# Mamba block and mixture of experts on one core: a new front and end, and a new order in the middle of each chunk

## The reference

```python
x = x + _layernorm(mamba(_layernorm(x)))
x = x + _layernorm(ffn(_layernorm(x)))

# mamba: 512 inner channels, 16 states, 4 taps
xz = x @ W_in; x_in, z = split(xz)
u = silu(causal_conv4(x_in) + conv_b)
dt_lr, Bm, Cm = split(u @ W_xproj)              # 16, 16, 16
delta = softplus(dt_lr @ W_dt + b_dt)
h_t = exp(delta_t * A) * h_{t-1} + delta_t * u_t * B_t   # per channel and state
y = (sum over n of h * C + D_skip * u) * silu(z)
out = y @ W_out

# ffn: shared gate/up/down (256), and 8 experts of 128 with top-2 softmax weights
routed = sum over e of coef_e * (silu(x@gate_e) * (x@up_e)) @ down_e
```

## Time and profile before

| what | us |
|---|---|
| median of three runs (lowest, highest) | 2349.79 (2345.92, 2350.08) |
| the profiled execution | 2349.13 |
| its span, first to last instruction | 2347.3 |
| from the start to the first scan | 58.8 |
| the sixteen chunks of scans | 58.8 to 2247.5 |
| after the last scan | 99.8 |
| VectorE busy | 2151.0 (92%) |
| TensorE busy | 2069.7 (88%) |
| GpSimd busy | 1970.5 (84%) |
| ScalarE busy | 1643.2 (70%) |

### The profile page before, as it was taken

How to read it: one execution, slowest core, us unless ns; L and a number is a source line. 1 busy time by engine, 2 the same in 40 slices (tenths; PEclk the granted TensorE clock), 3 DMA queues, 4 the chain that set the end, 5 groups by cost and what they waited for, 6 DMA issues and landing times. The chain is left out here.

```text
span 2347.3 us, 30291 instructions
## 1 busy us (share of the span) xinstructions
PE 2069.7 (88%) x9216; PEld 1345.5 (57%) x9216; DVE 2151.0 (92%) x3048; ACT 1643.2 (70%) x2489; POOL 1970.5 (84%) x1630
## 2 busy tenths in 40 slices
PE   5678989999989899989989899999989899897967
PEld 2345565656656565665656556565656656565544
DVE  1999999999999999999999999999999999998950
ACT  4657777777777776777767687677778777775632
POOL 4677898989989898998979899898989989798844
PEclk8759999999999999999999999999999999997989
DMA  4111221111121111212121211221112121111201
GB/s 129 41 37 41 64 64 51 59 60 59 55 64 54 60 55 59 64 55 60 59 56 50 68 60 54 60 61 56 51 55 72 55 60 50 55 55 46 76 14 46
DMA packets 92947, 134.28 MB, mean 57 GB/s; under 512 B 12000, under 2 KB 42976, under 8 KB 92784
## 3 DMA queue, kind: packets, MB, share of 16 engines
q1 hardware_dynamic: 92784, 132.34, 18.8%
HBM read 123.13 MB, written 9.18 MB: 56 GB/s over the span
## 5 line engine op out<-in xcount | busy, mean ns | idle before, releaser
L817 DVE TENSOR_TENSOR_SCAN h<-d_a,carry,d_bu 128x512 f32<-128x512 f32 x1024 | 1261.0, 1267 | 52.9 <-ACT d_a L623 46.2
L1062 POOL TENSOR_TENSOR d_bu<-delta_u,b_rows 128x1024 f32<-128x1024 f32 x512 | 1202.5, 2359 | 4.6 <-issue 0.3
L623 ACT ACTIVATE d_a<-delta,a_neg 128x512 f32<-128x512 f32 x1024 | 697.4, 689 | 500.7 <-DVE h L817 495.2
L457 PE MATMUL ht<-ident,h 128*128 128x128 f32 x4096 | 611.5, 295 | 104.4 <-DVE y_t L827 97.2
L457 PEld LDWEIGHTS ht<-ident,h 128*128 128x128 f32 x4096 | 506.4, 151 | 337.4 <-issue 121.5
L827 DVE SCALAR_TENSOR_TENSOR y_t<-ht,c_t,y_t 128x512 f32<-128x512 f32 x896 | 621.2, 735 | 2.8 <-PE ht L457 2.4
L532 PE MATMUL ring<-x_t,w_gate_sb 128*128 128x512 f32 x640 | 324.8, 633 | 21.3 <-ACT delta L782 18.0
L559 PE MATMUL dn<-w_down_sb,up_hidden 128*128 128x256 f32 x1280 | 302.9, 379 | 1.7 <-POOL up_hidden L1122 1.7
L539 PE MATMUL ring<-x_t,w_up_sb 128*128 128x512 f32 x640 | 292.5, 600 | 12.4 <-ACT silu_gate L716 12.2
L1117 POOL TENSOR_TENSOR up_hidden<-silu_gate,up_hidden 128x512 f32<-128x512 f32 x160 | 204.3, 1277 | 109.0 <-ACT up_hidden L720 76.9
L559 PEld LDWEIGHTS dn<-w_down_sb,up_hidden 128*128 128x128 f32 x1280 | 236.0, 190 | 60.0 <-issue 31.8
(11 more groups left out here) (121 smaller groups left out, 2013.0 us busy)
## 6 DMA issues: line engine op xcount, KB each, us to landing
b_rows<-b_rows_hbm SPq DMA_DIRECT2D x256, 256.0 KB, 3.5
coef_rows<-coef_rows_hbm SPq DMA_DIRECT2D x128, 256.0 KB, 3.5
xa<-L_attn_x_in SPq DMA_DIRECT2D x16, 512.0 KB, 5.0
xr<-L_attn_x_in SPq DMA_DIRECT2D x16, 512.0 KB, 5.1
out<-xr SPq DMA_DIRECT2D x16, 512.0 KB, 2.9
w_in_sb<-L_attn_W_in_in SPq DMA_DIRECT2D x1, 1024.0 KB, 6.3
w_gate_sb<-L_ffn_experts_gate_in SPq DMA_DIRECT2D x2, 512.0 KB, 4.8
w_up_sb<-L_ffn_experts_up_in SPq DMA_DIRECT2D x2, 512.0 KB, 5.7
```

Source lines behind the costliest of these rows:

```text
L457: last = nc.tensor.transpose(HT[q % HTS][:, j * P:(j + 1) * P], H[:, (NS * c + n) % HS, j, a * P:(a + 1) * P], IDN[:, :])
L623: nc.scalar.activation(DA[i % DAS][:, :], DL[:, r, j, :], ACT.Exp, scale=ANEG[:, j, n:n + 1]).then_inc(ex.sem, 1)
L817: nc.vector.tensor_tensor_scan(H[:, (NS * s + n) % HS, j, :], DA[(n * J + j) % DAS][:, :], BU[:, (2 * n + j // 2) % 4, j % 2, :], CARRY[:, ...
L1062: nc.gpsimd.tensor_tensor(BU[:, (2 * n + h) % 4, :, :], DU[:, 2 * h:2 * h + 2, :], BB[:, n % 2, :].unsqueeze(1).to_broadcast([P, 2, T]), A ...
```

## The change

- **Start.** TensorE no longer waits for the constants at the start but makes 32 products of the identity with itself (`WARM`) as soon as the identity is made; the wait for the constants' loads stands ahead of the preparation of chunk 0. ScalarE's exp and VectorE's negation of A_log move there too. The statistics and the normalisation of the first xa need none of it. GpSimd's `before_chunk(0)` moves behind the first rstd.
- **Chunk 0's preparation.** All four z tiles are made in slot 9, in turn in the two down banks (two in slots 58 and 60 in the ring before), and all SiLUs stand together in slot 14. The taps of the fourth group are added by VectorE (`add_first_taps`) and not by GpSimd. The second chunk's xa is normalised ahead of the first softplus (slot 27, was 50).
- **Every chunk.** The gates of pair 2 (f = 2 and 3) are both in slot 20, ahead of the coefficients' transposes in that slot; those go to DN[1] and no longer to the ring, and the first down product waits for their copy. ScalarE copies x_dbl and the coefficients one slot sooner (18, 20). Pairs 2, 3 and 4 start in slots 20, 30, 40 (22, 32, 42), the softplus groups in 28 and 38 (30, 40), two of the statistics in 24 and 34 (26, 36), the mean in 44 (42).
- **End.** Chunk 14's output is normalised at the start of lo = 16, ahead of ScalarE's last states. For chunk 15 VectorE adds each quarter once it is normalised, and SyncE stores each quarter by itself.

```diff
-        PAIR_AT = (12, 22, 32, 42, 50)
+        PAIR_AT = (12, 20, 30, 40, 50)
+        GATE_AT = (12, 13, 20, 20, 30, 31, 40, 41, 50, 51)
-        DL_PE, DL_ACT = (28, 29, 38, 39), (30, 30, 40, 40)
-        XA_STATS, XA_MEAN, XA_RSTD, XA_NORM, XT_PE, XT_ACT = (16, 16, 26, 36), 42, 47, 50, 61, 62
+        DL_PE, DL_ACT = (26, 27, 36, 37), (28, 28, 38, 38)
+        XA_STATS, XA_MEAN, XA_RSTD, XA_NORM, XT_PE, XT_ACT = (16, 16, 24, 34), 44, 47, 50, 61, 62
-        SILU_FIRST = {14: SILU[14] + SILU[60][:2], 60: SILU[60][2:]}
+        SILU_FIRST = {14: SILU[14] + SILU[60]}
+        WARM = 32
...
         def gate_slot(f):
-            return PAIR_AT[f // 2] + f % 2
+            return GATE_AT[f]
         def up_slot(f):
-            return gate_slot(f) + 3
+            return PAIR_AT[f // 2] + f % 2 + 3
         def hf_slot(f):
-            return gate_slot(f) + 5
+            return PAIR_AT[f // 2] + f % 2 + 5
-        MIDDLE = ([("xd", 1, 0, 0), ("cf", -1, 0, 1)], [("dl", 1, 0, 0), ("dl", 1, 1, 1)],
+        MIDDLE = ([("xd", 1, 0, 0)], [("dl", 1, 0, 0), ("dl", 1, 1, 1)],
...
+                    if lo == CHUNKS + 1 and t == 0:
+                        for a in range(NT):
+                            sp.wait_ge(tail.sem, a + 1)
+                            sp.dma_start(tokens(out, r, half - 1)[:, a, :], XR[:, s % 2, a, :]).then_inc(out_st.sem, 16)
...
         def _(pe):
-            pe.wait_ge(consts.sem, 1)
-            pe.wait_ge(const_ld.sem, CONST_LOADS)
             pe.wait_ge(ident_made.sem, IDENT_MADE)
+            for i in range(WARM):
+                nc.tensor.matmul(HT[i % HTS][:, 0:P], IDN[:, :], IDN[:, :], start=True, stop=True)
...
+                if lo == -1:
+                    pe.wait_ge(const_ld.sem, CONST_LOADS)
...
                 if t == CF_PE:
                     pe.wait_ge(rt.sem, rt.at(c))
-                    pe.wait_ge(*ring_user_before(s, lo, "cf", 0))
-                    bank = ring_bank("cf", 0)
+                    pe.wait_ge(x1t.sem, x1t.at(c))
+                    bank = DN[1]
...
                 if f == 0:
                     pe.wait_ge(rt.sem, rt.at(c))
+                    pe.wait_ge(cff.sem, cff.at(c))
...
-                    if t == Z_PE[j]:
-                        if j < 2:
+                    if t == (Z_PE[j] if lo >= 0 else Z_PE[0]):
+                        if lo < 0 and j >= 2:
+                            pe.wait_ge(z_raw.sem, z_raw.at(c, j - 1))
+                        elif j < 2:
+                            pe.wait_ge(sz.sem, sz.at(s, j + 3))
                             pe.wait_ge(resid["o"].sem, resid["o"].at(s - 1, 2 * j + 2))
+                        bank = z_bank(j) if lo >= 0 else DN[j % 2]
...
         def _(act):
-            act.wait_ge(const_ld.sem, CONST_LOADS)
-            nc.scalar.activation(ANEG[:, :, :], ANEG[:, :, :], ACT.Exp).then_inc(a_exp.sem, 1)
-            act.wait_ge(consts.sem, 1)
+            act.wait_ge(zeroed.sem, 1)
+                    if lo == -1 and t == 0:
+                        act.wait_ge(const_ld.sem, CONST_LOADS)
+                        nc.scalar.activation(ANEG[:, :, :], ANEG[:, :, :], ACT.Exp).then_inc(a_exp.sem, 1)
+                        act.wait_ge(consts.sem, 1)
+                    if lo == CHUNKS and t == 0:
+                        normed_y(s - 2)
-                    if exists(lo - 2) and t == 2:
+                    if exists(lo - 2) and lo != CHUNKS and t == 2:
                         normed_y(s - 2)
-                    if exists(lo + 2) and t == XA_NORM:
+                    if exists(lo + 2) and t == (XA_NORM if lo != -1 else DL_ACT[0] - 1):
                         normed("xa", s + 2, XA, XA)
-                if t == CF_PE + 1:
+                if t == CF_PE:
                     act.wait_ge(full["cf"].sem, full["cf"].at(c))
-                if t == XD_PE + 1:
+                if t == XD_PE:
                     act.wait_ge(full["xd"].sem, full["xd"].at(c))
...
+                    if lo == CHUNKS + 1 and t == 0:
+                        for a in range(NT):
+                            dve.wait_ge(norm["y"].sem, norm["y"].at(s - 2, a + 1))
+                            nc.vector.tensor_tensor(XR[:, s % 2, a, :], XR[:, s % 2, a, :], YN[:, a, :], ALU.add)\
+                              .then_inc(tail.sem, 1)
+                    if lo == -1 and t == POOL_CONV:
+                        add_first_taps(s + 1, o, POOL_J)
...
+            def add_first_taps(c, o, j):
+                nc.vector.tensor_tensor(U[:, o, j, 0:TAPS - 1], U[:, o, j, 0:TAPS - 1], HEAD[:, j, :], ALU.add)\
+                  .then_inc(conv_last.sem, 1)
+                for i in range(TAPS - 1):
+                    k = TAPS - 2 - i
+                    back = TAPS - 1 - k
+                    dve.wait_ge(conv_last.sem, conv_last.at(c, i + 1))
+                    nc.vector.tensor_tensor(U[:, o, j, back:], U[:, o, j, back:], YD[:, k, back:], ALU.add)\
+                      .then_inc(conv_last.sem, 1)
...
-                    if prep and t == POOL_CONV:
+                    if prep and lo >= 0 and t == POOL_CONV:
                         add_taps(s + 1, o, POOL_J)
-                    if exists(lo + 2) and t == HEAD_POOL:
+                    if exists(lo + 2) and lo > -2 and t == HEAD_POOL:
+                        before_chunk(s + 2, r)
+                    if lo == -2 and t == XA_RSTD + 1:
+                        pool.wait_ge(const_ld.sem, CONST_LOADS)
                         before_chunk(s + 2, r)
```

More of the change, by code:

```diff
@@ L163, in mamba_moe_kernel @@
         shift = {w: stage(f"shift_{w}", n) for w, n in dict(xa=2, o=2, x1=2, y=2).items()}
-        stream = stage("stream", 1)
+        stream, tail = stage("stream", 1), stage("tail", NT)
         scan, add_c, carry = stage("scan", NS * J), stage("add_c", (NS - 2) * NT), stage("carry_s", NS)
@@ L252, in mamba_moe_kernel @@
         ring_free = {"yd": (yd, 1), "xt": (xt, 1), "xin": (conv, TAPS), "z": (sz, 1),
-                     "gt": (tg, 1), "up": (up, 1), "cf": (cff, 1), "xd": (xd, 1), "ct": (ct, 1),
+                     "gt": (tg, 1), "up": (up, 1), "xd": (xd, 1), "ct": (ct, 1),
                      "dl": (softplus, 1)}
@@ L271, in ring_user_before @@
                 before, part, kb, bank_before = RING_USE[at]
-                if bank_before == bank and 0 <= lo - back + part < CHUNKS:
+                first = 1 if before == "z" else 0
+                if bank_before == bank and first <= lo - back + part < CHUNKS:
                     if before == "xin" and kb == POOL_J:
@@ L379, in body @@
                         sp.dma_start(XA[:, :, :], following).then_inc(xa_ld.sem, 16)
-                    if exists(lo - 2) and t == Y_POOL + 2:
+                    if lo == CHUNKS + 1 and t == 0:
+                        for a in range(NT):
+                            sp.wait_ge(tail.sem, a + 1)
+                            sp.dma_start(tokens(out, r, half - 1)[:, a, :], XR[:, s % 2, a, :]).then_inc(out_st.sem, 16)
+                    if exists(lo - 2) and lo != CHUNKS + 1 and t == Y_POOL + 2:
                         result, added = tokens(out, r, half - 1), stream.at(s - 2)
@@ L399, in _ @@
                 body(s, s, s % 2, s // 2)
-            sp.wait_ge(out_st.sem, out_st.at(CHUNKS - 1))
+            sp.wait_ge(out_st.sem, out_st.at(CHUNKS - 2) + NT * 16)
         IDENT_MADE = 2 + E
@@ L575, in prep_part @@
                             pe.wait_ge(*ring_user_before(s, lo, "z", j))
+                        bank = z_bank(j) if lo >= 0 else DN[j % 2]
                         for k in range(KM):
-                            last = nc.tensor.matmul(z_bank(j)[:, :], WIN[:, k, DI + j * P:DI + (j + 1) * P],
+                            last = nc.tensor.matmul(bank[:, :], WIN[:, k, DI + j * P:DI + (j + 1) * P],
                                                     XT[:, k, :], start=(k == 0), stop=(k == KM - 1))
@@ L721, in ffn_part @@
                           .then_inc(up.sem, 1)
-                if t == CF_PE + 1:
+                if t == CF_PE:
                     act.wait_ge(full["cf"].sem, full["cf"].at(c))
-                    nc.scalar.activation(XD[ROW_K:ROW_K + E, o, :], ring_bank("cf", 0)[0:E, :],
+                    nc.scalar.activation(XD[ROW_K:ROW_K + E, o, :], DN[1][0:E, :],
                                          ACT.Copy).then_inc(cff.sem, 1)
@@ L770, in prep_part @@
                             act.wait_ge(full["z"].sem, full["z"].at(c, k + 1))
-                        raw = SZ[:, o, k, :] if k < 2 else ring_bank("z", k)[:, :]
+                        raw = SZ[:, o, k, :] if k < 2 else (z_bank(k) if lo >= 0 else DN[k % 2])[:, :]
                         nc.scalar.activation(SZ[:, o, k, :], raw, ACT.Silu).then_inc(sz.sem, 1)
-                if t == XD_PE + 1:
+                if t == XD_PE:
                     act.wait_ge(full["xd"].sem, full["xd"].at(c))
@@ L801, in _, with finish_constants @@
             nc.vector.memset(EPS4[:, :], EPS).then_inc(zeroed.sem, 1)
```

(25 more changed lines are left out.)

## The result

The changed kernel takes 2362.98 us, the median of four runs (2362.58 to 2363.44), beside 2349.37 for the kernel before on the same chip: a ratio of 1.0060 (95% interval 1.0047 to 1.0072). It is slower by 14 us, outside the predicted range of 2328 to 2345. The profiled execution took 2363.25 us and its span is 2361.5, 14.1 more than before.

The account below looks back on a forecast made before the run. VectorE was taken to pace the sixteen chunks, a serial chain through all engines the front and end. -11.7 - 0.45 - 2.7 + 1.5 = -13.3 took the span from 2347.3 to 2334.0, a time of 2336 us; range 2328 to 2345.

Parts of the forecast that it names:

- Front: Start to the third scan: that scan moves from 61.6 to 49.9, 11.7 us won, bounds 6 and 14.
- Slots 18 to 23: Every chunk: the second pair's gates fill TensorE's wait ahead of the coefficients' transposes; cost 0 and nothing won.
- cover of 1.4 us: Slots 20 to 22: state transposes ready 3.5 us after coef, VectorE asking for them at 4.9.
- that rival's 3 to 8: Sixteen chunks: with TensorE's pause filled, fewer slow stretches make VectorE wait; 3 to 8 us more won, 2330; chance 0.12.
- Pairs two slots sooner: Every chunk: moved pairs and softplus groups keep their distances, only the cover of stalls changes; +1.5 us, bounds 0 and +3.
- The stalls named: VectorE in every chunk: a stall of 0.38 us in slot 41 and none in slot 45.
- The low clock had the bounds -4 and +4: Middle: slow stretches of TensorE's clock fall differently after the pairs move; value 0 us, bounds -4 and +4.
- End: After the last scan: quarters added by VectorE and stored separately, -2.7 us; chunk 14's output normalised earlier, -0.45 us.
- 0.45 less: End: normalising chunk 14's output ahead of ScalarE's last states releases the last y_d transposes sooner, -0.45 us.
- The one on the slower side: Slot 20: gates at the low clock delay the state transposes, VectorE waits 2.4 us a chunk, 37 in all: 2373; chance 0.08.
- The sum: Whole kernel: -11.7 - 0.45 - 2.7 + 1.5 = -13.3 from the span of 2347.3 gives 2334.0, then 2335.9, say 2336.

Follow-up runs that it names:

- gates22: pairs_back with the second pair's gate products at slots 22 and 23 again, behind the coefficients' transposes, instead of both at slot 20: 2333.84 us (0.9939).
- pairs_back: The changed kernel with pairs 2 to 4, softplus groups, statistics and mean back in their old slots: 2330.28 us (0.9924).
- all48r: The changed kernel with C's transposes at 46, fifth pair at 48, mean at 42, rstd_xa at 43 and normalisation at 48: 2330.20 us (0.9919).
- fill48: The changed kernel with nine throw-away TensorE products, four behind C's transposes in slot 48 and five ahead of slot 50's gates: 2346.24 us (0.9988).
- ct46: The changed kernel with the transposes of C in slot 46 instead of 48: 2347.14 us (0.9994).
- fill_rstd43: fill48 with the mean moved from slot 44 to 42 and GpSimd's rstd_xa operations from slot 47 to 43: 2338.78 us (0.9954).
- ct46_rstd43: ct46 with the mean moved from slot 44 to 42 and GpSimd's rstd_xa operations from slot 47 to 43: 2335.16 us (0.9941).

## Why the prediction was wrong

**Front: right.** The order of time after, answering to the earlier trace rows:

```profile
1.80 10.23 PE L416 MATMUL ht<-ident 128*128 128x128 f32 x64 [1.80 <-POOL ranks L1027]
...
4.73 1.41 DVE L860 BATCH_NORM_STATS2 stats_xa<-xa 128x6 f32<-128x256 f32 x4 [3.31 <-DMA xa<-L_attn_x_in]
...
8.63 1.28 ACT L660 ACT_TABLE_LOAD   x1 [8.63 <-POOL mean_rstd_xa L1088]
...
13.94 3.67 PE L454 MATMUL ring<-x_t,w_in_sb 128*128 128x512 f32 x8 [0.79 <-ACT x_t L712]
...
27.03 2.14 DVE L995 TENSOR_TENSOR u<-u,y_d 128x511 f32<-128x511 f32 x3
...
30.88 3.60 PE L598 MATMUL ring<-u,w_xproj_sb 128*80 128x512 f32 x8
...
34.51 0.59 ACT L794 ACTIVATE x_dbl<-ring 80x512 f32<-80x512 f32 x1 [2.67 <-PE ring L598]
...
46.70 4.65 POOL L1105 TENSOR_TENSOR d_bu<-delta_u,b_rows 128x1024 f32<-128x1024 f32 x2
```

The warm-up ends at 12.0 (13.1 said), the first x_in product is done at 16.0 (16.8), x_dbl is copied behind z3 at 35.1 (35.7), and the third scan starts at 49.15 behind its d_bu, which is done at 49.0 (49.9 said): 12.4 us won for 11.7. Not in the sum was a table load of 1.28 us ahead of the first normalisation, which stood with the constants' exp at 0.73 before; it made xa ready at 12.0 and not 10.7, and the warm-up hid it. That this miss cost nothing is luck.

**Slots 18 to 23: right in cost.** No stall in slots 21 to 23, so the cover of 1.4 us sufficed. That nothing is won there left out what the prediction had itself put among its rivals: with the pause before the coefficients filled, the 3.3 us of low clock a chunk in slots 20 to 23 are gone, worth some 3.6 us by gates22, if they are real. In pairs_back, where hardly more than the order of slot 20 is new in the middle, the sixteen chunks take 2185.0 us and not 2188.7, near the lower edge of that rival's 3 to 8.

**Pairs two slots sooner: the step that failed.** The prediction said "Every step keeps its distance to its neighbours" and priced it at +1.5 us, bounds 0 and +3; by pairs_back it is +32.7, of which the low clock behind TensorE's pause is 16 to 17 and GpSimd's order, once that is cured, 7.5 to 12. The sentence holds among pairs 2 to 4 and their softplus groups. It doesn't hold at their end. The diff leaves four things where they were: the fifth pair (50), the transposes of C (48), rstd_xa (47) and the normalisation (50). Between the fourth pair and these a hole of two slots opened on TensorE, and on GpSimd the order of `hidden` and rstd_xa changed. The stalls named came along as told (0.39 us in slot 41, none in 45); the dear ones were new ones in slots 52 to 56, a place for which the prediction had no row. The low clock had the bounds -4 and +4 with the value 0; filling the pause won 16.7 us. Those bounds came from no row: the earlier trace rows gave chunk 2 a clock of 0.99, and the question where a new pause would stand was asked for slot 20 alone. all48r shows that the reasoning itself, cost nothing if the distances are kept, is right.

**End: right in the size of its own terms.** The rows after, answering to the earlier trace rows; the last is the page's group of the four stores (KB each, us to landing).

```profile
2356.81 1.94 ACT L669 ACTIVATE silu_gate<-dn,mean_rstd_y,rstd_y 128x256 f32<-128x256 f32 x4 [9.75 <-POOL mean_rstd_y L1085]
2357.41 1.80 DVE L887 TENSOR_TENSOR xr<-xr,silu_gate 128x256 f32<-128x256 f32 x4 [2.55 <-ACT silu_gate L669]
...
out<-xr SPq DMA_DIRECT2D x4, 128.0 KB, 1.8
```

From the start of the last normalisation to the end of the span it was 7.7 us and is 4.65: 3.0 won for 2.7, the store landing in 1.8 us where 2.2 was taken. (The prediction's own times, 2346.9 less 2344.3, give 2.6.) From the last scan to that normalisation it is 0.7 us more (92.84 for 92.15) and not 0.45 less. TensorE's clock is low there for longer, 13.7 us from 2284.4 to 2298.1 where it was 10.2 (2270.1 to 2280.3); that this is the cause was not tried.

**The rivals.** The one on the slower side had its price nearly right (37 us in the middle) and its place wrong, slot 20. The mechanism it describes, state transposes that come late at the low clock, is the one that decided, three pairs later, at the fifth pair's gates, behind a pause that the change made and not behind one that it filled.

**The sum.** Its last step names the 0.7 us between the profiled execution and the median but doesn't add them: 2334.0 + 1.83 + 0.7 is 2336.5 and not 2335.9. Of the 27 us between forecast and result this is nothing; they are the middle, +29.0 for +1.5.

## What to carry to other kernels

When a block of work is moved, list what stands directly behind it on every engine and does not move: there the hole opens, and there the order flips. Then look in the trace for a stretch in which an in-order engine has no slack (here TensorE busy 14.92 of 14.95 us and GpSimd 14.65) and ask what fills it after the move. Causes that lie beside each other hide each other: curing GpSimd alone won 1.1 us, curing it behind the other 7 to 12, so a fix that does nothing is no proof that its cause isn't there.

## What the runs showed of the hardware

- Two pauses of 1.22 and 1.40 us, with transposes alone between them, came with 6.83 us at 1.2 GHz in eight chunks and 3.41 us in five, which began between the two or just behind the second; in the fifteenth chunk, with pauses of 0.57 and 1.40 us, the clock stayed at 2.4 GHz. In fill48 nine throw-away products in the same place held 2.4 GHz in all chunks from the second to the fifteenth. In ct46 TensorE pauses too, for 1.07 us ahead of the state transposes and for 0.63 us behind the first gate, and there the clock stays up in 11 of these 14 chunks. The Trainium skill, "TensorE: Matmul & The Clock Gate", section "Part 4: PE-mode transpose", says that transposes don't count as work for the gate. The three runs agree with that as well as with the pauses alone; none separates the two, since no run put transposes in the place of the fill.
- The low clock's price isn't its duration: 6.83 us at half speed made VectorE wait twice, 1.3 us in the seventh chunk, because the state transposes stand in TensorE's queue behind four gate records that took 1.8 us longer. Over chunks 2 to 15 fill_rstd43 has 116.1 us of low clock and the kernel before 116.7; both have none of it in slots 48 to 55, and their sixteen chunks take 2191.8 and 2188.7 us. The changed kernel has 160.5, and its chunks take 2217.7.
- At the end of the program the 128 KB stores landed in 1.8 us, where the 512 KB store took 2.9. Size alone doesn't set it: the 32 KB store of x_dbl's rows landed in 1.6 us before and in 3.0 (median) in the changed kernel. There it is issued one slot sooner, 0.75 us behind a 256 KB load (503.30 and 502.55 in the fourth chunk), and lands 0.17 us after that load; before it was 2.5 us behind (510.98 and 508.51) and landed 0.77 us after it. GpSimd's d_bu, which read these rows, stood idle 4.4 us in all and not 4.6, so it cost nothing there.
